# Last two blocks' rounds shared two to a sum, and 24 tiles of the layer norm closed with 65 columns

## What is computed

```python
e = concat(pu * (diag_u[:, None] * x[:2048] @ W_u) + x[:2048],
           pi * (diag_i[:, None] * x[2048:] @ W_i) + x[2048:])
h = adj @ (adj.T @ e)                      # adj is 5120 x 5120
out = (h - mean(h)) * rsqrt(var(h) + 1e-5) * gamma + beta + x
y = layernorm(x + out)
result = layernorm(y + second_layer(y, adj))
```

## Time and profile before

| | before |
|---|---|
| median of 3 runs | 397.51 us (397.47 to 397.99) |
| the profiled execution | 398.1 us |
| its span, first to last instruction | 396.2 us |
| mean granted TensorE clock | 0.991 of full speed |
| busy in the span: TensorE, VectorE, ScalarE, GpSimd | 96%, 80%, 68%, 16% |
| DMA | 109.83 MB, mean 277 GB/s |

### The profile page before, as it was taken

One profiled execution on the slowest core, in us unless ns is written; L12 is line 12 of the kernel. 1 busy time (PEld: TensorE's weight loads), 2 busy tenths in 40 slices (PEclk: granted clock), 3 DMA queues, 4 the chain that ended last, 5 costly groups with the idle time before them and its releaser, 6 DMA issues.

```text
span 396.2 us, 13302 instructions
## 1 busy us (share of the span) xinstructions
PE 379.4 (96%) x5762; PEld 220.5 (56%) x5762; DVE 316.6 (80%) x305; ACT 268.6 (68%) x519; POOL 63.9 (16%) x125
## 2 busy tenths in 40 slices
PE   8987999999999999999999999999999999999980
PEld 7643556465456546545654664565466456555770
DVE  1699799797879869797976989697698869795674
ACT  3597995896968668587857858685876778501143
POOL 2000300300200300030030003003000300277375
PEclk9999999999999999999999999999999999999996
DMA  7999999994798789679877957996895799300012
GB/s 284 387 387 379 387 386 385 322 381 158 266 378 302 261 283 392 216 274 391 317 262 260 392 203 275 392 345 215 290 387 192 274 393 376 144 3 2 24 35 85
DMA packets 56991, 109.83 MB, mean 277 GB/s; under 512 B 3808, under 2 KB 4576, under 8 KB 56928
## 3 DMA queue, kind: packets, MB, share of 16 engines
q1 hardware_dynamic: 56640, 108.84, 76.1%
q10 hardware_dynamic: 288, 0.09, 0.1%
HBM read 107.60 MB, written 1.31 MB: 275 GB/s over the span
## 4 chain that ended last, share of the span: by engine, by line
PE 86%; SPq 8%; DMA 3%; DVE 1%; POOL 1%; issue 1%; POOLq 0%; ACT 0%
PE quad L1485 45%; PE quad L1465 39%; SPq L1028 6%; DMA pooled<-in_adj 3%; PE quad L1500 2%; SPq L1019 1%; DVE pooled L1280 1%; POOL pooled L1107 1%; SPq L1014 1%; POOLq L98 0%; POOL pooled L1102 0%; SPq L1020 0%; DVE pooled L1333 0%; DVE pooled L1373 0%; ACT pooled L1178 0%
## 5 line engine op out<-in xcount | busy, mean ns | idle before, releaser
L1260 DVE STREAM_TRANSPOSE pooled<-pooled 128x1024 f32<-128x1024 f32 x200 | 229.8, 1208 | 8.0 <-ACT scratch L1148 8.0
L1148 ACT ACTIVATE scratch<-pooled 128x1024 bf16<-128x1024 f32 x200 | 210.0, 1051 | 37.3 <-DMA pooled<-in_adj 35.4
L1465 PE MATMUL quad<-pooled,rows_in 128*64 128x256 f32 x1600 | 180.7, 381 | 4.0 <-DMA pooled<-in_adj 3.9
L1485 PE MATMUL quad<-pooled,col_sum 32*64 32x320 f32 (+4 forms) x3968 | 177.5, 507 | 0.6 <-issue 0.2
L1465 PEld LDWEIGHTS quad<-pooled,rows_in 128*64 128x64 f32 x1600 | 111.8, 137 | 74.5 <-issue 12.5
L1485 PEld LDWEIGHTS quad<-pooled,col_sum 32*64 32x64 f32 x3968 | 88.0, 132 | 82.8 <-issue 63.7
L1280 DVE TENSOR_TENSOR pooled<-pooled,quad 128x1280 f32<-128x1280 f32 (+5 forms) x29 | 52.4, 1808 | 42.9 <-PE quad L1485 42.9
L1079 POOL COPY col_sum<-col_half 32x256 f32<-32x256 f32 x80 | 31.6, 394 | 312.4 <-DVE col_half L1269 309.5
L1157 ACT COPY col_sum<-col_half 32x256 f32<-32x256 f32 x80 | 32.3, 403 | 41.3 <-DVE col_half L1269 40.5
L1148 ACT ACTIVATION_READ_ACCUMULATOR scratch<-pooled 128x1 f32 x200 | 37.4, 187 | 0.0
L1178 ACT ACTIVATE pooled<-quad 128x256 f32<-128x256 f32 (+2 forms) x7 | 3.3, 476 | 23.4 <-PE quad L1500 23.4
(11 more groups left out here) (48 smaller groups left out, 62.8 us busy)
## 6 DMA issues: line engine op xcount, KB each, us to landing
pooled<-in_adj SPq DMA_DIRECT2D x200, 512.0 KB, 9.3
pooled<-in_x SPq DMA_DIRECT2D x5, 256.0 KB, 3.9
pooled<-in_x SPq DMA_DIRECT2D x1, 768.0 KB, 5.2
pooled<-in_x SPq DMA_DIRECT2D x1, 512.0 KB, 3.7
out<-pooled SPq DMA_DIRECT2D x2, 256.0 KB, 2.6
out<-pooled SPq DMA_DIRECT2D x2, 192.0 KB, 2.8
out<-pooled SPq DMA_DIRECT2D x3, 128.0 KB, 2.1
pooled<-in_w_ui ACTq DMA_DIRECT2D x1, 64.0 KB, 3.3
```

The lines of the kernel that those rows point to most:

```text
L1148: nc.scalar.activation(scratch[v % 2][:, :], slots[slot_of(v)], ACT.Square, accum_out=square_sum[:, v:v + 1]).then_inc(unit_scanned, 1)
L1260: nc.vector.transpose(tiles, tiles).then_inc(unit_turned, 1)
L1465: mm = pe.matmul(block_bank(c)[half(h), 0:w // 2], rows_in[:, t, :], slots[slot_of(v)][:, at:at + w // 2], start=(t == 0), stop=(t == T - 1))
L1485: mm = pe.matmul(round_banks(g)[a][half(b % 2), 0:w].rearrange("p (t r) -> p t r", r=32), col_sum[c % 2][quadrant(a), b, :], to[quadrant(a ...
```

## The change

Three parts.

**Rounds.** Blocks 8 and 9 both have rounds of 16, 16 and 8 tiles. They alternate from `JOINED` on: (8, 0, 16), (9, 0, 16), (8, 16, 16), (9, 16, 16), (8, 32, 8), (9, 32, 8). Two consecutive ones accumulate in the same banks as one sum; VectorE adds the pair once. No round stands between units 16 and 17 of block 9 any more. x is read again after (8, 0, 16). The norm's banks are now the upper four.

**Closing.** The first three groups (24 tiles, `NARROW`) are closed with 65 columns: 64 give the centered features, the 65th the mean of the features times gamma. Two new VectorE instructions in `take_c` multiply by a row of gamma and subtract the 65th column; `scale_y` then reads their result. The other groups keep 128 columns. For this there is one more small load (`gamma_row`, 128 partitions of 64 values), two small VectorE instructions beside those that prepare gamma, and one more column copied by ScalarE.

**Groups.** `NORM_PARTS` has 8, 8, 8, 8, 4 and 4 tiles, and every engine's order in the norm is written anew.

```diff
-    PARTS = [((0, 10), (10, 14), (24, 16))] * (NB - 1)
-    PARTS += [((0, 12), (12, 12), (24, 8), (32, 8))]
+    PARTS = [((0, 10), (10, 14), (24, 16))] * (NB - 2)
+    PARTS += [((0, 16), (16, 16), (32, 8))] * 2
...
+    ORDER = [(c,) + part for c in range(NB - 2) for part in PARTS[c]]
+    JOINED = len(ORDER)
+    ORDER += [(c,) + part for part in PARTS[NB - 1] for c in (NB - 2, NB - 1)]
...
-    NORM_PARTS = ((0, 6), (6, 6), (12, 4), (16, 8), (24, 8), (32, 4), (36, 4))
+    NORM_PARTS = ((0, 8), (8, 8), (16, 8), (24, 8), (32, 4), (36, 4))
...
-    BY_ACT, BY_DVE = (1, 2, 3), (0, 4, 5, 6)
-    SHORT = 5
+    BY_ACT, BY_DVE = (1, 2), (0, 3, 4, 5)
+    SHORT = 4
+    NARROW = 3
...
+            if g >= JOINED:
+                return banks_of_block(NB - 2) == (g < JOINED + 2)
...
+        def opens_sum(g):
+            return g < JOINED or (g - JOINED) % 2 == 0
+        def ends_sum(g):
+            return g < JOINED or (g - JOINED) % 2 == 1
...
SyncE
+                    sp.dma_start(gamma_row[:, :], gamma.rearrange("d o -> (d o)").partition_broadcast(P)).then_inc(norm_in, 16)
...
-            sp.wait_ge(round_done, ROUNDS_AT[NB - 2] + 1)
+            sp.wait_ge(round_done, JOINED + 1)
             for a, b in ((0, USER_TILES), (USER_TILES, T)):
                 sp.dma_start(x_all[:, a:b, :], tile_rows(x, a, b - a)).then_inc(x_again, 16)
...
GpSimd
-            for k in range(LGROUPS):
+            for k in range(LGROUPS - 1):
                 center_x(k)
+            root_c(0)
+            center_x(LGROUPS - 1)
...
(then root_c(1), root_y(0), root_c(2), root_y(1), root_c(3), root_y(2), root_c(4), root_c(5), root_y(3), root_y(4), root_y(5))
...
ScalarE
+                    act.copy(center[:, 2 * D:2 * D + 1], bank[3][:, D:D + 1]).then_inc(center_kept, 1)
...
(square_c(0), square_y(0), square_c(1), square_c(2), square_y(1), square_c(3), square_y(2), make_out(1), square_c(4), square_y(3), square_c(5), make_out(2), square_y(4), square_y(5))
...
VectorE
+            def take_c(k):
+                nt = norm_size(k)
+                dve.wait_ge(c_squared, k + 1)
+                if k == 0:
+                    dve.wait_ge(gamma_steps, 1)
+                nc.vector.tensor_tensor(ln_t[k % 2][:, 0:nt, :], features_of(k),
+                                        gamma_row[:, :].unsqueeze(1).to_broadcast([P, nt, D]), ALU.mult).then_inc(c_scaled, 1)
+                dve.wait_ge(c_scaled, k + 1)
+                nc.vector.tensor_tensor(ln_t[k % 2][:, 0:nt, :], ln_t[k % 2][:, 0:nt, :],
+                                        nat_of(k)[:, 0:nt, D:D + 1].to_broadcast([P, nt, D]),
+                                        ALU.subtract).then_inc(nat_taken, 1)
...
-            for v in range(UNITS - 6, UNITS - 4):
+            for v in range(UNITS - 6, UNITS):
                 turn_unit(v)
...
+            add_round(JOINED + 1)
             dve.wait_ge(eps_put, 4)
             sum_c(0)
+            take_c(0)
...
             make_y(0)
+            survives = edges_may_survive(dve)
+            add_round(JOINED + 3)
+            sum_c(1)
+            take_c(1)
             sum_y(0)
+            sum_c(2)
+            take_c(2)
+            make_y(1)
             make_out(0)
+            sum_y(1)
             make_y(2)
+            sum_c(3)
             sum_y(2)
+            scale_y(3)
+            add_tiles(NR - 1, *NORM_PARTS[NORMS - 2])
+            add_tiles(NR - 1, *NORM_PARTS[NORMS - 1])
+            add_x(3)
             sum_c(4)
+            sum_c(5)
             sum_y(3)
+            make_y(4)
+            make_y(5)
             sum_y(4)
             sum_y(5)
+            make_out(3)
             make_out(4)
             make_out(5)
...
TensorE
-                                       start=(b < 2), stop=(b >= kb - 2))
+                                       start=(b < 2 and opens_sum(g)), stop=(b >= kb - 2 and ends_sum(g)))
...
-                if k >= 2:
+                if k >= 2 + NARROW:
                     pe.wait_ge(t_made, k - 1)
+                elif k >= 2:
+                    pe.wait_ge(nat_taken, k - 1)
+                kinds = slice(D, 2 * D + 1) if k < NARROW else slice(0, 2 * D)
...
+            multiply_round(JOINED)
+            multiply_round(JOINED + 1)
+            multiply_round(JOINED + 2)
             close_tiles(0)
             pe.wait_ge(max_found, 1)
             pe.matmul(max_bank()[0:1, 0:P], part_max[:, :], ident[:, :], start=True, stop=True).then_inc(max_found, 1)
+            multiply_round(JOINED + 3)
             close_tiles(1)
             close_tiles(2)
+            multiply_round(JOINED + 4)
             close_tiles(3)
+            multiply_round(JOINED + 5)
             close_tiles(4)
             close_tiles(5)
```

More of the change, by code:

```diff
@@ L142, in adjacency_layers_kernel @@
         ln_o = [ln_buffer(D) for _ in range(4)]
-        assert ln_at <= x_at + CH * PARTS[NB - 2][0][1] and ln_end[0] <= x_at + CH * sum(PARTS[NB - 2][1])
+        assert ln_end[0] <= x_at + CH * PARTS[NB - 2][0][1]
         rows_in = sb("rows_in", [P, T, D])
@@ L374, in upper_banks, with sums_through @@
             c = place_of_round(g)[0]
-            if c == NB - 1:
-                return banks_of_block(NB - 2) == (g != LAST)
-            return banks_of_block(c) == (c == NB - 2 or g < ROUNDS_AT[c + 1] - 1)
+            if g >= JOINED:
+                return banks_of_block(NB - 2) == (g < JOINED + 2)
+            return banks_of_block(c) == (g < ROUNDS_AT[c + 1] - 1)
+        def opens_sum(g):
+            return g < JOINED or (g - JOINED) % 2 == 0
+        def ends_sum(g):
+            return g < JOINED or (g - JOINED) % 2 == 1
+        def sums_through(g):
+            return sum(1 for r in range(g + 1) if ends_sum(r))
         def round_banks(g):
@@ L406, in added_through @@
             first, nt = NORM_PARTS[k]
-            g = rounds_through(NB - 1, first + nt - 1)
-            return g if g < NR else NR - 1 + sum(1 for f, _ in NORM_PARTS[:k + 1] if f >= place_of_round(NR - 1)[1])
+            g = rounds_through(NB - 1, first + nt - 1) - 1
+            if g < NR - 1:
+                return sums_through(g)
+            return sums_through(g - 1) + sum(1 for f, _ in NORM_PARTS[:k + 1] if f >= place_of_round(g)[1])
         def turned_of(g):
@@ L1042, in store_made @@
                 store_out(sp, k)
-            for k in (0, 1, 2, 4, 5, 3, 6):
+            for k in (0, 1, 2, 3, 4, 5):
                 store_made(k)
@@ L1459, in multiply_unit @@
                     same = before_in_banks(ROUNDS_AT[c - 1], banks_of_block(c))
[L1460 removed]
+                    pe.wait_ge(round_added, sums_through(same[-1]))
                 for k in range(ut):
```

127 lines of the change are left out of this document (49 added, 78 removed).

## The result

The changed kernel takes 404.33 us (median of 4 runs, 404.08 to 404.6), the kernel before 397.49 beside it (397.34 to 397.99). The ratio is 1.0161 [1.0148, 1.0175]. The profiled execution took 404.54 us, its span is 402.7 against 396.2, and the mean granted clock 0.979 against 0.991. The forecast was 397.8, in a range up to 398.9.

What follows compares the result with a forecast made beforehand. TensorE's unbroken run plus a tail bounds the kernel; after the change VectorE may decide. Addition of tiles 32 to 35 +0.37, tail 0, stores -0.1: +0.3 us on 397.51, thus 397.8, range 396.6 to 398.9.

Steps and rivals of the forecast that it cites:

- The forecast's own path: End of the norm: VectorE, not TensorE, delays adding tiles 32 to 35, by 0.85 us; closes' gain lost in waits; chance 0.53.
- The load of gamma's row: Early units, where TensorE waits for each: one more small load costs 0.1 us (0 to 0.2), not given back.
- The narrow close: Closes with 65 columns: 1.1 us for 8 tiles (1.04 to 1.9); the 24 tiles save 2.6 us of TensorE.
- the third rival: Narrow closes save nothing, since the stationary operand loads as before; 399.1 us, or 398.4 at 0.2 a tile; chance 0.08.
- The chain of x: First round's end to make_y(0): 22.3 us, VectorE free 0.3 before the second sum; rival that it comes late, chance 0.14.
- The clock: Rival: granted clock falls in the new waits of 1.4 and 1.7 us, last closes 2.3 us longer, 400; chance 0.03.
- The last units' wait for DMA: Before the rounds, last units of block 9: 0.8 us of new waiting (0.4 to 1.0), the last unit landing late.
- The three rounds: Rounds up to close 0: three of 512 columns at 13.6 ns a column take 20.9 us.
- VectorE's pitches from the second addition on: VectorE from the second sum: 0.60 us between 512-element operations, 0.72 if dependent; 11.4 us to 381.1.
- Its wait for GpSimd's root before scale_y(3): VectorE after sum_c(3), before adding tiles 32 to 35: 0.9 us of waiting for the root of 8 tiles.
- The tail: From the addition of tiles 32 to 35 to the last multiplication: unchanged at 9.14 us.
- the stores: After the last multiplication: last three stores have 512 KB instead of four with 768; 0.1 off 3.98 us (0 to 0.3).

Runs made afterwards that it cites:

- e2: The kernel before, with only the load of gamma_row added where the changed kernel has it: 400.17 us, ratio 1.0049.
- e16: The kernel before, with one more small plain load (gamma to 64 partitions, 4 bytes each) behind beta's: 397.89 us, ratio 1.0004.
- e17: The kernel before, with gamma_row's load in place of beta's and beta's four units later: 398.02 us, ratio 1.0014.
- e18: The kernel before, with gamma_row's load one unit behind beta's instead of directly behind it: 398.82 us, ratio 1.0029.
- e4: The kernel before, with each group's 8 products of x reordered, first the even tiles, then the odd ones: 403.12 us in one run.
- e3: The changed kernel, with GpSimd's last centering of x waiting until VectorE has made y of group 0: 402.26 us, ratio 1.009.
- e7: The changed kernel with 128 columns in every close and without take_c's VectorE instructions, gamma_row's load kept: 399.86 us, ratio 1.004.
- e12: The changed kernel, all closes 128 columns wide, plus two 1024-element VectorE copies before the second addition to lengthen TensorE's wait: 404.14 us, one run.
- e1: The changed kernel, with gamma_row's load issued by ScalarE's queue at the kernel's start instead of by SP: 403.44 us, ratio 1.0126.
- e6: The changed kernel, with gamma_row's load moved ahead of block 3 and the row scaled after the last unit: 402.33 us, ratio 1.012.
- e11: The changed kernel, narrow closes kept, gamma_row's load ahead of block 3 and GpSimd's first root after three centerings: 398.01 us, ratio 1.0008.
- e5: The changed kernel, with its first joined round (8, 0, 16) put back between units 16 and 17 of block 9: 407.43 us, ratio 1.0245.
- e8: The changed kernel with 128-column closes, no gamma_row load, and the first joined round between units 16 and 17 of block 9: 403.5 us, ratio 1.0145.
- e9: The changed kernel with 128 columns in all closes and no gamma_row load, leaving joined rounds and six groups: 398.34 us, ratio 0.9997.
- e10: The changed kernel with 128-column closes, no gamma_row load, and GpSimd's first root after three centerings instead of four: 397.78 us, ratio 0.9992.

## Why the prediction was wrong

The forecast's own path didn't decide. VectorE was to come 0.85 us behind TensorE with tiles 32 to 35, with waits of 1.4 us before close 2 and 1.7 before close 4. In the changed kernel these waits are 2.31 and 0.85, and TensorE decides as before, because three things held TensorE up before it got there.

**The load of gamma's row**, taken at 0.1 us (0 to 0.2): 2.44. The step that failed is the comparison with the earlier trace rows, where gamma and beta cost one 0.1. They were one spread over the partitions and one plain, and a second load of the same kind right behind the first is no further case of it. e2, e16, e17 and e18 show this. It alone takes the time out of the range.

**The narrow close**, taken at 1.1 us for 8 tiles (1.04 to 1.9): 1.93, so the third rival's mechanism was true, to which I gave 0.08. I took the value of the earlier trace rows because it has the same stationary columns. One unlike part was which rows of the array the tiles use: e4 shows that this is 0.46 of the 0.89 us between the earlier trace rows and a narrow close, and the rest stays open. The Trainium skill ("TensorE: Matmul & The Clock Gate", section "LDWEIGHTS (loading the stationary operand)") gives a load a price by its columns alone, from which I had estimated 0.21 us a tile. The measured 0.24 for narrow and 0.25 for wide closes lie near it, somewhat above. I had let overrule it. The Trainium skill says in the same page's section "Step-by-step: what each phase is for" that a load is pulled ahead when the row groups don't conflict, or when it goes to a background buffer. The first fits with 0.13 a tile and e4 with 0.19; of the second no run here tells anything.

**The chain of x**, taken to be in time with 0.3 us to spare: 1.75 late (374.35 against 372.6). From the end of the first round to the end of y it was to take 22.3 us and took about 25.2. Two terms failed. The second load of x landed 6.3 us after its issue, not 5.2 as in the earlier trace rows (the page's DMA issues: count, size, us to landing):

```profile
pooled<-in_x SPq DMA_DIRECT2D x1, 768.0 KB, 6.3
```

And scale and add took 371.28 to 374.42, 3.1 us instead of 1.4, since in the changed kernel both read SBUF twice, beside GpSimd. Against both stood the 0.3 us to spare, and that close 0 was 0.8 longer, which gave the chain that much more room. The four centerings (9.8, predicted 9.9), the root (1.68) and the sum (2.8) were right. The Trainium skill ("SBUF — State Buffer", section "Who interferes with whom") says that a VectorE instruction with two inputs in SBUF contends with a GpSimd instruction that reads SBUF, that the lock is exclusive, and that the order of issue decides who blocks. The traces agree for the centerings: here VectorE's two instructions start 0.13 and 0.50 after GpSimd's and take 1.47 and 1.64 with the end 0.55 after GpSimd's, 0.69 when GpSimd stands still (e3), 0.69 when one input is in PSUM (e7). Beside GpSimd's roots nothing of it is to be seen: L1392 at 382.95 begins during a root (381.79 to 383.43) and takes 0.68. Moving the product with gamma to VectorE is what took that input out of PSUM, and the prediction costed `scale_y` by rows that read PSUM.

**The clock**, which had 0.03: it fell around both new waits. The early fall cost nothing, since the units landed no sooner; the late one cost 2.7. I read from the earlier trace rows that it holds for about 3 us after TensorE stops. Here it was down within 1.6 us (stopped 374.37, half by 376), in e12 after 2.3, in e1 and e6 after 2.4 and 2.9, when close 2 was already running, and in e3 likewise, after 1.07 us of idle time. One instance of a delay was no lower bound.

**What was right.** The last units' wait for DMA: 0.74, predicted 0.8, and e6 starts its rounds at 339.99. The three rounds: 20.78, predicted 20.9. VectorE's pitches from the second addition on, though it then stood still for 1.87 us, for the slow close 2. Its wait for GpSimd's root before scale_y(3) is 1.15, predicted 0.9. The tail: 8.86, predicted 9.14; the stores gained more than the 0.1 taken, 0.89. Repaired (e11, 398.01 beside 398.12 for the kernel before), the change does what the forecast of +0.3 us said, within the uncertainty, though that is luck in part, since errors cancel: closes 0.8 longer each, stores 0.9 shorter.

The rivals were each worked out as if the others didn't happen. Late x, wide closes and clock came together: the late x made the wait, and around the wait the clock fell.

## What to carry to other kernels

When a row is taken as the price of a new operation, ask what its instances share besides the shape: which rows of the array they use, whether their inputs are in PSUM or SBUF, what runs on GpSimd beside them, and what stands ahead of them in the queue. A thin cover behind a serial chain isn't worth its mean: what is late there makes TensorE idle, and a fallen clock can cost more than the wait. Put small loads that spread a row over the partitions into a stretch in which the queue waits for slots anyway, and apart from each other.

## What the runs showed of the hardware

- Two loads spread over 128 partitions, issued 0.6 us apart in a queue that carries some 385 GB/s, held the next unit back by 2.95 to 3.31 us in five kernels (changed, e2, e3, e5, e7) and by 2.07 in e12; one such load 0.1, a plain small one nothing, and one 512 KB load between them 1.5.
- Eight products on 64 rows of the array each took 1.04 us with the halves in turn and 1.50 without.
- Before close 2 the granted clock fell to half around waits of 1.07, 1.93, 2.26, 2.31 and 3.00 us, and not around 0.47 to 0.69, nor around 1.38 with wide closes. Elsewhere it fell around waits of 2.95 to 3.31 (the late unit), 3.14 (e4), 4.15 and 4.17 (e5, e8), and not around 1.53 (e18) and 2.07 (e12). In e4 it also fell at 12.92, with no wait over 0.33 us since TensorE's first product. So the length of one wait doesn't decide it.
- A VectorE instruction with both inputs in SBUF that met a GpSimd centering of 512 elements a partition ended 0.55 us after it, whatever its own start; a root of 8 did not hold it up (0.68). Also in e7 (L1399 at 373.57, ended 374.30; GpSimd's ended at 373.75).
- The second load of x (768 KB) landed 5.1 to 5.4 us after its issue in eight kernels in which it is issued 1.2 to 4.0 us after the last unit landed (before, e2, e4, e5, e8, e16, e17, e18), and 5.9 to 6.8 in nine where 8.3 us had passed (the changed kernel, e1, e3, e6, e7, e9, e10, e11, e12). What went before in the queue is one difference between them; the cause wasn't tried.
